# A two-layer model kernel: one addition and one ratio per unit, first sums scaled by ScalarE, and the second output's and the gate's products moved to GpSimd

## What is computed

```python
def bi_wkv(r, k, v, w, u, time_emb):          # used twice, with r = x and k = v = f
    tf = sigmoid(sum(time_emb, -1))
    decay = exp(-exp(w)) * (0.5 + 0.5 * tf)
    ek = exp(minimum(k, 30)); ekv = ek * v
    nf, df = forward recurrences  a = a * decay + ekv,  b = b * decay + ek
    nb, db = the same two, backward over the tokens
    euk = exp(minimum(u + k, 30))
    num = nf + nb - ekv + euk * v
    den = df + db - ek + euk
    return sigmoid(r) * (num / maximum(den, 1e-8)) * (0.8 + 0.2 * tf)

x = x + attn(bi_wkv(x, f, f, w1, u1, cond))   # attn: inp, decay and gate are three 512x512 products of its input,
                                              # state = decay * state + (1 - decay) * inp over the tokens,
                                              # (gate * state) @ W_out + b_out
x = x + ffn(bi_wkv(x, f, f, w2, u2, cond))    # ffn: the two best of 8 experts per token, 512 -> 2048 -> 512, relu,
                                              # at most 640 tokens an expert
```

## Time and profile before

| | |
|---|---|
| median of 3 runs | 1221.15 us (1221.03 to 1222.53) |
| the execution that was profiled | 1220.83 us, of which the span in the trace is 1218.7 us |
| granted TensorE clock, mean over the span | 0.954 of full speed |
| PE busy | 1040.2 us, 85% |
| VectorE (DVE) busy | 683.5 us, 56% |
| ScalarE (ACT) busy | 526.5 us, 43% |
| GpSimd (POOL) busy | 312.7 us, 26% |

### The profile page before, as it was taken

How to read it: one execution, slowest core, us unless ns; L and a number is a source line. 1 busy time by engine, 2 the same in 40 slices (tenths; PEclk the granted TensorE clock), 3 DMA queues, 4 the chain that set the end, 5 groups by cost and what they waited for, 6 DMA issues and landing times.

```text
span 1218.7 us, 17577 instructions
## 1 busy us (share of the span) xinstructions
PE 1040.2 (85%) x5058; PEld 828.1 (68%) x5059; DVE 683.5 (56%) x1016; ACT 526.5 (43%) x882; POOL 312.7 (26%) x251
## 2 busy tenths in 40 slices
PE   1126879778799829999999999999999999999994
PEld 0012335434348529998999899989898888999883
DVE  6989999899881633334333433345555344343553
ACT  5354557647654222334233423344545334333553
POOL 3785837737730330000200200020201101100202
PEclk9999988988989859999999999999999999999997
DMA  5251250211010443113411521282635234311711
GB/s 191 104 166 34 81 174 35 69 70 69 0 71 35 174 160 118 69 69 115 109 69 69 147 78 69 69 206 99 191 138 184 85 130 136 86 69 69 215 70 21
DMA packets 63405, 125.28 MB, mean 103 GB/s; under 512 B 4726, under 2 KB 4762, under 8 KB 63384
## 3 DMA queue, kind: packets, MB, share of 16 engines
q1 hardware_dynamic: 54728, 107.91, 25.4%
q0 software_dynamic: 8656, 17.13, 6.9%
HBM read 93.04 MB, written 35.22 MB: 105 GB/s over the span
## 4 chain that ended last, share of the span: by engine, by line
PE 58%; issue 1%; ACT 1%; DVE 1%; DVEq 1%; POOL 0%; ACTq 0%; POOLq 0%
PE ps_y L1136 10%; PE ps_y L1137 10%; PE ps_y L1138 10%; PE ps_h L1116 9%; PE ps_h L1118 9%; PE ps_h L1117 9%; PE ps_t L1086 1%; POOL out_dram L1065 0%; ACT xh L1231 0%; ACT y L1238 0%; DVEq L1176 0%; DVE hl L1293 0%; ACT w1h L1203 0%; DVE y L1308 0%; DVE w1l L1254 0%
## 5 line engine op out<-in xcount | busy, mean ns | idle before, releaser
L1116 PE MATMUL ps_h<-xh,w1h 128*128 128x320 f32 (+3 forms) x768 | 247.7, 322 | 7.4 <-issue 3.2
L1118 PE MATMUL ps_h<-xh,w1l 128*128 128x320 f32 (+3 forms) x768 | 243.7, 317 | 0.0
L1117 PE MATMUL ps_h<-xl,w1h 128*128 128x320 f32 (+3 forms) x768 | 243.5, 317 | 0.0
L1065 POOL DMA_INDIRECT out_dram<-y,token x40 | 64.6, 1614 | 657.4 <-ACT y L1238 489.6
L1293 DVE SCALAR_TENSOR_TENSOR hl<-ps_h,hh 128x320 fp32r<-128x320 f32 (+1 forms) x192 | 106.8, 558 | 194.1 <-ACT hh L1227 189.3
L1136 PE MATMUL ps_y<-w2h,hh 128*128 128x512 f32 x528 | 206.6, 391 | 1.9 <-DVE hl L1293 1.9
L1137 PE MATMUL ps_y<-w2h,hl 128*128 128x512 f32 x528 | 206.8, 392 | 0.0
L1138 PE MATMUL ps_y<-w2l,hh 128*128 128x512 f32 x528 | 206.3, 391 | 0.0
L1257 DVE TENSOR_TENSOR w2l<-raw,w2h 128x512 fp32r<-128x512 f32 x128 | 88.5, 692 | 196.8 <-ACT w2h L1206 196.8
L1227 ACT ACTIVATE hh<-ps_h 128x320 fp32r<-128x320 f32 (+1 forms) x192 | 94.3, 491 | 230.9 <-PE ps_h L1118 230.8
L1206 ACT ACTIVATE w2h<-raw 128x512 fp32r x128 | 80.8, 631 | 211.5 <-PE ps_y L1138 211.5
(11 more groups left out here) (197 smaller groups left out, 1277.1 us busy)
## 6 DMA issues: line engine op xcount, KB each, us to landing
raw<-in_L_ffn_w_dram SPq DMA_DIRECT2D x64, 1024.0 KB, 7.2
slots<-r_rows SPq DMA_DIRECT2D x8, 1302.5 KB, 15.6
rows<-slots SPq DMA_DIRECT2D x8, 1302.5 KB, 8.2
f_rows<-in_fside_BxSxS_dram SPq DMA_DIRECT2D x5, 1024.0 KB, 5.3
rows<-in_x_dram SPq DMA_DIRECT2D x4, 1024.0 KB, 6.1
out_dram<-x_rows SPq DMA_DIRECT2D x4, 1024.0 KB, 5.6
slots<-r_rows POOLq DMA_DIRECT2D x1, 1302.5 KB, 6.5
rows<-slots SPq DMA_DIRECT2D x5, 260.5 KB, 3.6
```

Of the source, the lines that this page charges most:

```text
L1116: nc.tensor.matmul(o, w1h[:, j, dt, :], xh[:, dt, lo:hi], start=(dt == 0), stop=False)
L1117: nc.tensor.matmul(o, w1h[:, j, dt, :], xl[:, dt, lo:hi], start=False, stop=False)
L1118: last = nc.tensor.matmul(o, w1l[:, j, dt, :], xh[:, dt, lo:hi], start=False, stop=(dt == CT - 1))
```

## The change

Six edits. (1) L802 and the table `inv_pair` go; ScalarE multiplies the first elements by `inv_md2` in two small activations per unit, one for each c, placed between the reciprocal of the previous unit and the exponentials of the next one. VectorE's forward scans wait for them. (2) The two additions L813 become one of 1024 elements. (3) The two ratios of a unit become one instruction of 1024 elements, with one array `ratios` for both results; those of unit 3 stay two. (4) The second output's product in stages 2 and 3 goes to GpSimd, behind the products of unit 2, as a plain product; in stages 4 and 5 it stays on VectorE. (5) Its scale factor is applied later: in the copy of the logits and in the copies of the rows on ScalarE. (6) The product of gate and state of stages 1 to 3 goes to GpSimd, behind the last newton of the stage; in stage 4 it stays on VectorE.

```diff
@@ gpsimd
+        def second_out(b):
+            pool.wait_ge(s_sig2, b + 1)
+            pool.wait_ge(s_ratio, 2 * CT * (b + 1))
+            g.tensor_tensor(sig[:], ratio_of(b, 1), sig[:],
+                            ALU.mult).then_inc(s_r2, 1)
+
+        def gated(b):
+            for e in range(CT):
+                pool.wait_ge(s_rec_steps, 2 * CT * b + 2 * (e + 1))
+                g.tensor_tensor(z_gate[:, e], z_gate[:, e], z_in[:, e], ALU.mult).then_inc(s_y, 1)
...
                 if s < CT:
                     products(b * CT + (s + 1), (s + 1) % CT)
+                if s == 1 and at_least(b, 2):
+                    second_out(b - 2)
+            if at_least(b, 1):
+                gated(b - 1)
@@ scalar
+        def first_sums(b, ct):
+
+            u, r = b * CT + ct, ct % 2
+            for c in range(2):
+                act.wait_ge(s_bwd, 2 * u + c + 1)
+                act.nop(nofuse=True)
+                a.activation(sums[r][:, c, :, 0], sums[r][:, c, :, 0], ACT.Copy,
+                             scale=inv_md2[:, col(b, c, ct)]).then_inc(s_first, 1)
...
-            a.activation(r2_rows[:, i, 0:C], row_bank(i, banks)[:], ACT.Copy).then_inc(s_ev_r2, 1)
+            act.nop(nofuse=True)
+            a.activation(r2_rows[:, i, 0:C], row_bank(i, banks)[:], ACT.Copy,
+                         scale=neg_scale[:, bass.ds(b, 1)]).then_inc(s_ev_r2, 1)
...
                     if s >= 1:
                         first_reciprocal(b, s - 1)
+                    first_sums(b, s)
                     exps(b if s + 1 < CT else b + 1, (s + 1) % CT)
@@ vector, fold
-            steps = Steps(dve, s_fold, 5 * u)
-            dve.wait_ge(s_bwd, 2 * u + 2)
-            first = sums[r][:, :, :, 0]
-            steps.do(v.tensor_tensor(first, first, inv_pair[:, bass.ds(b * CT + ct, 1)].rearrange("p b c o -> p (b c) o")
-                                     .to_broadcast([P, 2, 2]), ALU.mult))
+            steps = Steps(dve, s_fold, 3 * u)
             for c in range(2):
+                dve.wait_ge(s_first, 2 * u + c + 1)
...
-            for c in range(2):
-                steps.mark(v.tensor_tensor(sums[r][:, c, 1], sums[r][:, c, 1], euk[:, r, c], ALU.add))
-            steps.wait()
+            steps.do(v.tensor_tensor(sums[r][:, :, 1], sums[r][:, :, 1], euk[:, r], ALU.add))
@@ vector, ratio
-            v.scalar_tensor_tensor(out=(r1T, ratio2)[c][:, bass.ds(b % 2, 1), ct, :],
-                                   in0=sums[r][:, c, 1].rearrange("p (o t) -> p o t", o=1), scalar=2.0,
-                                   in1=sums[r][:, c, 0].rearrange("p (o t) -> p o t", o=1),
-                                   op0=ALU.subtract, op1=ALU.mult).then_inc(s_ratio, 1)
+            v.scalar_tensor_tensor(out=ratios[:, bass.ds(b % 2, 1), cs, ct, :].rearrange("p o c t -> p (o c) t"),
+                                   in0=sums[r][:, cs, 1], scalar=2.0, in1=sums[r][:, cs, 0],
+                                   op0=ALU.subtract, op1=ALU.mult).then_inc(s_ratio, cs.stop - cs.start)
@@ vector, recurrence
-                v.tensor_tensor(z_gate[:, e], z_gate[:, e], z_in[:, e], ALU.mult).then_inc(s_y, 1)
+                if gated_here:
+                    v.tensor_tensor(z_gate[:, e], z_gate[:, e], z_in[:, e], ALU.mult).then_inc(s_y, 1)
@@ vector, second_out and select
-            v.scalar_tensor_tensor(out=sig[:], in0=ratio2[:, bass.ds(b % 2, 1)].rearrange("p o c t -> p (o c) t"),
-                                   scalar=neg_scale[:, bass.ds(b, 1)], in1=sig[:],
-                                   op0=ALU.mult, op1=ALU.mult).then_inc(s_r2, 1)
+            v.tensor_tensor(sig[:], ratio_of(b, 1), sig[:],
+                            ALU.mult).then_inc(s_r2, 1)
...
-            st.do(v.tensor_copy(logit[:], ps_logit))
+            st.do(v.tensor_scalar(logit[:], ps_logit, neg_scale[:, bass.ds(b, 1)], None, ALU.mult))
@@ vector, order
-                if tail and s == 1:
+                if tail and s == 1 and not cond:
                     second_out(b - 2)
...
-                    ratio(b, s - 1, 0)
-                    ratio(b, s - 1, 1)
+                    ratio(b, s - 1, slice(0, 2))
             if cond:
-                ratio(b, CT - 1, 0)
+                ratio(b, CT - 1, slice(0, 1))
             if gates:
-                recurrence(b - 1)
+                recurrence(b - 1, not cond)
             if cond:
                 first_out(b)
-                ratio(b, CT - 1, 1)
+                ratio(b, CT - 1, slice(1, 2))
```

More of the change, by code:

```diff
@@ L155, in conditioning_and_routing @@
     inv_md2 = sb("inv_md2", [P, B * 2 * CT])
-    inv_pair = sb("inv_pair", [P, B * CT, 2, 1])
     own_bias = sb("own_bias", [P, (B + 1) * 2 * CT])
@@ L172, in conditioning_and_routing @@
     recip0 = sb("recip0", [P, 2, T])
-    r1T = sb("r1T", [P, 2, CT, T])
-    ratio2 = sb("ratio2", [P, 2, CT, T])
+    ratios = sb("ratios", [P, 2, 2, CT, T])
+    ratio_of = lambda b, c: ratios[:, bass.ds(b % 2, 1), c].rearrange("p o n t -> p (o n) t")
     sig = sb("sig", [P, CT, T])
@@ L219, in conditioning_and_routing @@
     s_own = sem("numerator_own_term")
+    s_first = sem("first_sums_scaled")
     s_gh, s_gl = sem("gate_operands_high"), sem("gate_operands_low")
@@ L242, in gate_piece @@
         high, low = gate_parts[2 * which:2 * which + 2]
-        raw = r1T[:, (B - 1) % 2, dt, :] if which == 0 else wm[:, which, dt, :]
+        raw = ratios[:, (B - 1) % 2, 0, dt, :] if which == 0 else wm[:, which, dt, :]
         return raw, high[:, dt], low[:, dt]
@@ L437, in gate @@
                 last = nc.tensor.matmul(ps_mm[:, k % 3, :], wm[:, m, dt, e * P:(e + 1) * P],
-                                        r1T[:, bass.ds(b % 2, 1), dt, :].rearrange("p o t -> p (o t)"),
+                                        ratios[:, bass.ds(b % 2, 1), 0, dt, :].rearrange("p o t -> p (o t)"),
                                         start=(dt == 0), stop=(dt == CT - 1))
@@ L774, in _ @@
         setup.mark(v.tensor_scalar(den_min[:], inv_md2[:], DEN_MIN, None, ALU.mult))
-        for c in range(2):
-            setup.mark(v.tensor_copy(inv_pair[:, :, c].rearrange("p (b t) o -> p b (t o)", b=B),
-                                     inv_md2[:].rearrange("p (b c t) -> p b c t", b=B, c=2)[:, :, c]))
         dve.wait_ge(s_setup_a, 4)
@@ L817, in fold, with ratio @@
             last.then_inc(s_den, 1)
-        def ratio(b, ct, c):
+        def ratio(b, ct, cs):
             u, r = b * CT + ct, ct % 2
-            dve.wait_ge(s_newton, 2 * u + c + 1)
+            dve.wait_ge(s_newton, 2 * u + cs.stop)
             if ct == 0 and at_least(b, 2):
-                dve.wait_ge(*((s_mm, 12 * (b - 1)) if c == 0 else (s_r2, b - 1)))
-            v.scalar_tensor_tensor(out=(r1T, ratio2)[c][:, bass.ds(b % 2, 1), ct, :],
-                                   in0=sums[r][:, c, 1].rearrange("p (o t) -> p o t", o=1), scalar=2.0,
-                                   in1=sums[r][:, c, 0].rearrange("p (o t) -> p o t", o=1),
-                                   op0=ALU.subtract, op1=ALU.mult).then_inc(s_ratio, 1)
+                dve.wait_ge(s_mm, 12 * (b - 1))
+                dve.wait_ge(s_r2, b - 1)
+            v.scalar_tensor_tensor(out=ratios[:, bass.ds(b % 2, 1), cs, ct, :].rearrange("p o c t -> p (o c) t"),
+                                   in0=sums[r][:, cs, 1], scalar=2.0, in1=sums[r][:, cs, 0],
+                                   op0=ALU.subtract, op1=ALU.mult).then_inc(s_ratio, cs.stop - cs.start)
         def first_out(b):
@@ L833, in first_out, with recurrence @@
             dve.wait_ge(s_ratio, 2 * CT * (b + 1) - 1)
-            r1 = r1T[:, bass.ds(b % 2, 1)].rearrange("p o c t -> p (o c) t")
+            r1 = ratio_of(b, 0)
             v.scalar_tensor_tensor(out=r1, in0=r1, scalar=neg_scale[:, bass.ds(b, 1)], in1=sig[:],
                                    op0=ALU.mult, op1=ALU.mult).then_inc(s_r1, 1)
-        def recurrence(b):
+        def recurrence(b, gated_here):
             steps = Steps(dve, s_rec_steps, 2 * CT * b)
```

## The result

The changed kernel takes 1227.80 us (median of 5 runs, 1226.82 to 1229.58) where the kernel before, run beside it, takes 1221.15 (1220.95 to 1222.53): 1.0055 times as long, 95% interval 1.0043 to 1.0067. It is 6.65 us slower. The forecast was 1217.3 with a range to 1226; only rival C was on this side. The execution profiled took 1229.58 us with a span of 1227.8, the slowest of the five.

The account below looks back on a forecast made before the run. VectorE was taken to bound stages 0 to 3, PE the experts after them. Terms -3.4 - 0.6 - 2.7 - 1.65 + 2.0 + 1.4 + 1.1 = -3.85 us gave 1217.3 against the median 1221.15; range 1208 to 1226.

Parts of the forecast that it names:

- rival C: Slower: GpSimd's queue becomes the bound in stages 2 and 3, if unit 1's Newton ends after 30; 1226.6 us; chance 0.18.
- stage 0 and change-over 0 to 1: Fewer alternations and L802 gone give -3.4 us in stage 0; last ratio no longer meeting products gives -0.6 at the change-over.
- stage 1: L802 gone and one addition: unit 0 -0.3, unit 1 -1.0, units 2 and 3 together -1.4; -2.7 us.
- change-over 1 to 2: Recurrence 2 us longer from gate products on GpSimd, but later conditioning products slow it less; net -1.65 us.
- stage 2: Unit 0 gains 0.4, unit 3 closes 1.4 later behind GpSimd's work; +1.0 us, bounds -2.1 to +3.3.
- change-over 2 to 3: Longer recurrence from gate products on GpSimd, without the relief of the change-over before; +1.4 us.
- stage 3: Same replay as stage 2, with the output product in GpSimd's queue; +1.0 us.
- close of unit 3 to the first projection: After stage 3, the first y on GpSimd stands behind the next tile's L843: 3.7 instead of 2.6 us, +1.1.
- collision with the routing selection: Stages 2 and 3: five tiny VectorE instructions each stand behind one GpSimd instruction; 3.1 us become 6.4.
- rival B: The recurrence's scan is free of GpSimd, sign L845 staying at 1.22; 1211.4 us, down to 1205; chance 0.24.
- The relief from 1 to 2: Conditioning products that stretched L835 to 3.35 us where 2.34 do would come later, outweighing the 2 us longer recurrence.
- Rival D: What is moved comes back: ScalarE scales late or the alternation eats the rest; 1220 to 1222 us; chance 0.16.

Follow-up runs that it names:

- first_quarter: Changed kernel with output product cut: VectorE multiplies channel tile 0 just ahead of the ratio overwriting it, GpSimd the other three; 1223.31 us, 1.0025 of the kernel before.
- copies_first: Changed kernel with both products back on VectorE and ScalarE's copies of gate sums 3, 4, 5 and x2 rows 3 ahead of unit 2's scaling; 1209.20 us.

## Why the prediction was wrong, point by point

The sum of the forecast beside what the same stretches did in the changed kernel's profile, in us (minus is a gain; a stage runs from its first backward scan to the close of unit 3):

| term | forecast | measured |
|---|---|---|
| stage 0 and change-over 0 to 1 | -4.0 | -4.0 |
| stage 1 | -2.7 | -2.3 |
| change-over 1 to 2 | -1.65 | -0.5 |
| stage 2 | +1.0 | +3.6 |
| change-over 2 to 3 | +1.4 | +3.1 |
| stage 3 | +1.0 | +4.6 |
| close of unit 3 to the first projection | +1.1 | +1.5 |

With the later start of 0.2 us the right column gives the +6.22 of the first projection. The miss lies in stages 2 and 3 and between them.

- **First sums to ScalarE.** The step that failed: "The exponentials of the next unit now stand behind a wait for this unit's backward scans; GpSimd's products need them about one unit later, so I cost that at nothing". It looked at the next instruction in ScalarE's queue and its consumer, and not at the copies for PE further back. In both_back, the kernel without either product on GpSimd, putting these copies ahead of the wait gained 1220.04 - 1209.20 = 10.8 us, of which 8.2 lie before the first projection; in the changed kernel the same order gained 6.9 us (7.3 by the mark). The gain that the forecast had from L802 is there only in part. The two kernels with copies first that differ by the scaling are 8.3 us apart (1217.46 and 1209.20), near L802's 8.6 us of busy time, but only 6.5 us of that come before the first projection: 2.3 in stage 0, 3.6 in stage 1 and 0.4 in stage 2 (each with its change-over), 0.1 in stage 3, and 0.2 of start. The other 1.7 us fall behind it, where nothing is scaled, so that the 8.3 lie near the 8.6 is in part luck. In stages 2 and 3 unit 1 closes at 14.3 us after unit 0 with L802 and without it, as the forecast's replay had it. VectorE waited for the scaling itself for at most 0.44 us a time in the changed kernel.
- **Merges and scaling, stages 0 and 1.** Right. Stage 0 with its change-over gained 4.0 (forecast 4.0), stage 1 took 45.5 us from the close of unit 0 to that of unit 3 (forecast 44.5 to 46), unit 1 of stage 2 closed at 14.33 us after unit 0 (forecast 14.4).
- **Output product to GpSimd.** The duration was right (4.4 forecast, 4.51 measured) and so was its place in the queue. The step that failed: "VectorE starts the backward scans of unit 2 at 16.65". They start at 22.46, after 5.90 us of reuse wait. The step asked what stands behind the product on GpSimd, and not who else waits for its semaphore. The edit that removes that wait gave 4.2 us in first_quarter. The forecast's collision with the routing selection (214.19 to 217.24 us) did not come, because GpSimd was then waiting for the reciprocals of unit 2:

```profile
222.13 1.27 POOL L355 TENSOR_TENSOR sums_even<-sums_even,recip 128x512 f32<-128x512 f32 x1 [6.52 <-ACT recip L607]
```

- **Gate product to GpSimd.** Direction right, rival B wrong: the recurrence's scan does contend. In the change-over from stage 1 to 2 it takes 2.17 us for 1.22. From 2 to 3 and after stage 3 it stays at 1.22, which the forecast had named as the sign that B is right; there the product keeps out the next tile's first operation (L862, 1.77 us for 0.69) instead, and the step is 3.15 us all the same (forecast 3.0). Two terms were mis-sized. The relief from 1 to 2: +2.0 - 3.65 was forecast, and the stretch gained only 0.5. And the change-over from 2 to 3: +1.4 was forecast and +3.1 measured. In profiles with copies first the product costs 1.5, 2.2 and 0.6 us at the three places, 4.3 in sum. Rows of VectorE in the changed kernel at the first place and at the last, then GpSimd's at the last:

```profile
153.97 2.17 DVE L864 TENSOR_TENSOR_SCAN z_in<-z_dec,z_in 128x512 f32<-128x512 f32 x1
...
342.59 1.77 DVE L862 SCALAR_TENSOR_TENSOR z_in<-z_dec,z_in 128x512 f32<-128x512 f32 x1
344.39 1.23 DVE L864 TENSOR_TENSOR_SCAN z_in<-z_dec,z_in 128x512 f32<-128x512 f32 x1
```

```profile
342.54 1.26 POOL L367 TENSOR_TENSOR z_gate<-z_gate,z_in 128x512 f32<-128x512 f32 x1 [1.89 <-DVE z_in L864]
```

- **Rival C** had the sign and nearly the time (1226.6), for another reason. GpSimd's queue was not full: in stage 2 it waited 6.52 us in one piece and its Newton of unit 1 ended at 28.5, before the 30 from which C decides. What set the time was in no engine's replay: ScalarE's order (7.3 us by the first projection) and the reuse wait (4.2).
- **Rival D** was right for the products, and for the scaling only as the change placed it (both_back came to 1220.04, in its 1220 to 1222, though VectorE hardly waited for the scaling itself, and the copies behind the scaling did it). The rule that the forecast cites, in the Trainium skill, Perfetto Trace Analysis, "Optimizing Scalar/DVE Operations", is not about ScalarE: it says that VectorE and GpSimd share an SBUF read port. The runs agree for that pair and go beyond "might not help": 4.7 us of output products taken off VectorE cost 5.1 us of kernel time with the reuse wait, and three quarters of them without that wait still 3.1; some 7 us of gate products cost 6.8 by the medians and 4.3 by the profile. What was moved to ScalarE gained 6.5 us by the first projection, once its order was mended.

## What to carry to other kernels

When an instruction with a new wait is put into an engine's queue, list everything behind it up to the end of that wait, for every consumer, PE's transposes and copies too; then put what does not need the wait ahead of it. When a reader of a reused buffer moves to another engine, look for the writer that used to be ordered behind it for nothing. In this kernel work moved off VectorE to GpSimd cost more than it saved each time. Work moved to ScalarE paid in stages 0 and 1 and gave almost nothing in stages 2 and 3, although VectorE was nearly as full there before (46.90 of 48.53 us in stage 2), so what a microsecond off a full engine is worth has to be read stage by stage.

## What the runs showed of the hardware that was not expected

A GpSimd instruction keeps contended VectorE work out for its own length, not for a fixed 1.1 us: beside a 128x1536 product (3.88 us) a 128x1024 ratio took 4.06 us instead of 1.22. Whether the same product cut into short ones would be a better neighbour was not tried.

PE's granted clock enters where it was not looked for. both_back's twelve runs lie in two groups, 1217.65 to 1219.29 and 1220.80 to 1221.71 us, with a clock over the whole run of 0.953 to 0.955 in the first and 0.949 to 0.950 in the second. The profiled one is of the second; its windows around the logits after stage 3 (start and end, length, PE, PEld, VectorE, ScalarE, GpSimd busy, granted clock), and then those of the kernel before:

```profile
330.00:372.64 42.64, 37.75 (x105) 19.41 (x105) 28.62 (x44) 20.99 (x33) 11.97 (x10) 0.92 0.20 75
372.64:382.00 9.36, 9.36 (x47) 8.52 (x46) 2.25 (x19) 1.37 (x2) 0.00 (x0) 0.64 0.00 0
```

```profile
330.00:374.95 44.95, 37.31 (x105) 19.27 (x106) 29.34 (x45) 24.68 (x36) 14.28 (x12) 0.89 0.19 71
374.95:382.00 7.05, 7.05 (x53) 6.51 (x52) 2.19 (x19) 1.43 (x3) 0.00 (x0) 1.00 0.00 1
```

PE was busy without a break in both windows that start with the logits. In both_back the clock fell during the logits and stood at 0.50 (1.2 GHz) from 375 to 380 us. The logits took longer, and so did the wide gate products behind them. The window and two timeline rows of both_back, then the logits of the kernel before:

```profile
375.00:380.00 5.00, 5.00 (x21) 4.61 (x21) 2.25 (x19) 0.69 (x1) 0.00 (x0) 0.50 0.00 0
```

```profile
372.64 4.68 PE L492 MATMUL ps_small<-wg,sig 128*128 128x8 f32 x32
...
379.34 0.63 PE L442 MATMUL ps_mm<-r_high,w_decay_high 128*128 128x512 f32 x1
```

```profile
374.95 3.63 PE L481 MATMUL ps_small<-wg,sig 128*128 128x8 f32 x32
```

At the full clock such a gate product takes 0.39 us. From the first projection to the first expert matmul it took 122.86 us in both_back instead of 119.45. The changed kernel's profiled run has such a stretch too (0.50 from 385 to 390 us) and took 122.48 us; copies_first has a shorter one and took 118.81. So a part of the 10.8 us between the medians of both_back and copies_first is this tail, and where a comparison turns on a few microseconds, the first projection is given beside the medians. What decides whether, and for how long, the clock drops there was not tried.
